# Routing of a two-layer graph and expert kernel done row tile by row tile

## The chip, the cores and the metric

The kernel runs on one core of one Trainium2 chip. The core has five engines that run side by side: PE (matrix multiplies), DVE (vector), ACT (activations, here also copies and a DMA queue), POOL (general, here also indirect DMA) and SP (which only issues DMAs). PE works on clocks that are granted to it, 2.4 GHz or 1.2 GHz. The metric is the device time of one execution in microseconds, the median of several.

## What is computed

N = 3327 nodes with D = 256 features, a dense 0/1 adjacency matrix, E = 8 experts of which each node takes two.

```python
x = x + L0_gnn(layernorm(x), adj)   # softmax(x @ node_w) * softmax(where(adj > 0, h @ h.T, -big)), times adj, @ (x @ weight) + bias
x = x + L0_ffn(layernorm(x))        # top 2 of x @ Wg + bg; (silu(x @ W1) * (x @ W3)) @ W2 by expert, H = 512
x = x + L1_gnn(layernorm(x), adj)   # relu((adj @ x) @ W.T + b)
x = x + L1_ffn(layernorm(x))        # top 2 of x @ gate_w.T; gelu(x @ w1.T + b1) @ w2.T + b2 by expert, H = 1024

top_vals, top_idx = top_k(logits, 2)
gates = softmax(top_vals)           # y[node] = sum over its two experts of gate * expert(x[node])
```

## The kernel before

The nodes stand in T = 26 row tiles of P = 128 (the last has 127 rows). The program is a list of stages; at the end of each (`Stage.end`) all five engines meet at a barrier, so no engine starts on a stage before the slowest has left the one ahead. The order of the instructions is written out by hand, an engine at a time, and semaphores tie the engines together; `tiles` unrolls the first tiles and the last and loops over the rest two at a time. The stages are

- `project`: layernorm and the three projections. SP also turns both gate weights to expert-major rows in DRAM (`a["turned"]`).
- `attend`: for each row tile the scores against all nodes in seven chunks (PE L624), masked by DVE (L548), the exponential on ACT (L515); then in seven groups PE turns the probabilities (L633), ACT copies them as the high part (L521), DVE takes the low part (L533), and PE multiplies both with the support rows (L659, L661, the last one L664). The scores of tile t+1 run ahead of the groups of tile t.
- `route` (name gate0), `experts` (ffn0), `normalize`.
- `neighbours`: for each row tile PE turns the mask in four parts (L1417), ACT and DVE copy it (L1476, L1509), PE multiplies it with the normed nodes (L1424), turns the sum (L1433, function `finish` of PE) and projects it (L1439); DVE's `finish` adds bias, applies relu, adds x and takes the row statistics (L1519 to L185).
- `route` (gate1), `experts` (ffn1), `copy_out`.

The class `Gate` is called by both loops. POOL norms a finished row tile (L199 to L211), SP stores it to `xn`, and DVE forms the eight logits as eight products with sums over 256 columns (L224, `sums`) and adds the bias (L230) into `LG`, which holds all logits until `route`. In `attend` the eight sums of tile t−1 stand in twos between the low parts of the groups of tile t; in `neighbours` all eight of tile t−3 stand between the second and the third copy of the mask.

`route` then works on all 3328 x 8 logits at once: top two, gates, a count of the pairs before each pair (PE L804, L805), a place for every pair, and an inversion of that list by one-hot multiplies (L813), which yields `r["tok"]`, `r["dst"]`, `r["of_pair"]` and `r["expert"]` for S = 59 tiles of 128 pairs, sorted by expert. Meanwhile SP issues the weights: in gate0 16 pieces of w_in (L973) and w_out in one (L976); for ffn1 the pieces of w_in are issued in the neighbours loop, w_out and the biases in gate1.

`experts` takes the 59 tiles in turn: POOL gathers 128 rows of `xn` by token (L1063), PE turns them (L1101), ACT copies them (L1160, `copy_x`), DVE takes the low part (L1232), PE multiplies (L1112, L1136), and POOL adds the result to the rows of x (L1076). `xn` rows are 258 wide, since the two gates of a node ride behind its features.

## Time and profile before

| | us |
|---|---|
| median of 3 runs | 1818.52 |
| lowest, highest | 1814.2, 1821.43 |
| the profiled execution | 1819.35 |
| span of its profile | 1817.8 |
| PE, DVE, POOL, ACT busy in it | 1551.0, 1150.7, 698.9, 638.9 |

The span is the time between the first and the last instruction in the trace. The stages lie in it so: projection to 83 us, attention to 657, routing to 698, experts to 1026, normalize to 1066, neighbours to 1316, routing to 1357, experts to 1803, the copy of the output to the end. In a row of the timeline the first number is the start in us, the second the duration; a bracket says how long the engine stood idle ahead of it and what released it. A row with xN stands for N like instructions in a row.

### The profile page before, as it was taken

How to read it: one execution, taken by the hardware profiler on the slowest of the kernel's cores; microseconds unless marked ns; L12 is line 12 of the kernel's file. 1: busy time of each engine (PE TensorE's matmuls, PEld its weight loads, DVE VectorE, ACT ScalarE, POOL GpSimd, SP SyncE). 2: the span in 40 equal slices, each digit the busy share in tenths (PEclk: the TensorE clock that was granted, in tenths of full speed). 3: DMA queues.
4: the chain of work that ended last, by engine and by line, in shares of the span. 5: the costliest groups of instructions: out<-in, count | busy, mean ns of one | idle time of the engine just before them, and what ended most of it. 6: DMA issues, size and time to landing. Idle time of an engine off the chain costs nothing. (4 is left out here: it accounts for less than half of the span.)

```text
span 1817.8 us, 36040 instructions
## 1 busy us (share of the span) xinstructions
PE 1551.0 (85%) x9584; PEld 1291.5 (71%) x9584; DVE 1150.7 (63%) x3860; ACT 638.9 (35%) x1349; POOL 698.9 (38%) x1336
## 2 busy tenths in 40 slices
PE   5899999999999925999999339999618999999994
PEld 4888888888888724887888326555307888888894
DVE  5467777777777776566655346666685666666652
ACT  2333333333333301322223243222205565555562
POOL 0122322232222213776667204443414555455551
PEclk9899999999999966999999769999858999999997
DMA  6324344333334353333333424555341222222223
GB/s 94 111 109 150 136 145 151 132 130 130 130 132 146 98 196 114 51 49 49 52 49 50 98 94 153 195 205 195 110 189 30 41 35 38 38 35 36 40 37 91
DMA packets 85363, 184.70 MB, mean 102 GB/s; under 512 B 19790, under 2 KB 62540, under 8 KB 81292
## 3 DMA queue, kind: packets, MB, share of 16 engines
q1 hardware_dynamic: 57386, 128.02, 21.6%
q0 software_dynamic: 22656, 31.07, 11.2%
q10 hardware_dynamic: 5280, 25.17, 3.5%
q8 instruction: 14, 0.23, 0.1%
q14 instruction: 27, 0.21, 0.0%
HBM read 132.66 MB, written 54.99 MB: 103 GB/s over the span
## 5 line engine op out<-in xcount | busy, mean ns | idle before, releaser
L1112 PE MATMUL bank<-ffn_w_in_parts,ffn_x_t 128*128 128x512 f32 x1416 | 361.1, 403 | 1.7 <-DVE ffn_w_in_parts L1251 1.7
L1136 PE MATMUL bank<-ffn_w_out_parts,ffn_hidden_t 128*128 128x256 f32 x2124 | 285.0, 288 | 19.5 <-DVE ffn_hidden_t L1241 19.5
L1112 PEld LDWEIGHTS bank<-ffn_w_in_parts,ffn_x_t 128*128 128x128 f32 x1416 | 258.9, 190 | 55.9 <-DVE ffn_w_in_parts L1251 5.0
L1136 PEld LDWEIGHTS bank<-ffn_w_out_parts,ffn_hidden_t 128*128 128x128 f32 x2124 | 263.2, 192 | 25.1 <-issue 16.2
L624 PE MATMUL bank<-h_t,attn_h_tile 128*128 128x512 f32 (+1 forms) x1092 | 248.8, 383 | 3.9 <-POOL attn_h_tile L493 3.9
L659 PE MATMUL bank<-support,attn_probs_t 128*128 128x512 f32 x650 | 246.7, 413 | 5.1 <-DVE attn_probs_t L533 4.7
L624 PEld LDWEIGHTS bank<-h_t,attn_h_tile 128*128 128x128 f32 x1092 | 197.0, 189 | 46.1 <-issue 4.1
L521 ACT CAST attn_probs_t<-bank 128x512 fp32r<-128x512 f32 (+1 forms) x182 | 98.7, 557 | 357.5 <-PE bank L633 357.5
L1076 POOL DMA_INDIRECT x<-ffn_y,ffn_dst x118 | 196.5, 1665 | 53.6 <-issue 53.6
L1178 ACT ACTIVATE ffn_silu_or_gelu<-bank,w_b_in 128x128 f32<-128x128 f32 x472 | 134.6, 368 | 155.9 <-PE bank L1123 155.9
L661 PE MATMUL bank<-support,attn_probs_t 128*128 128x256 f32 x676 | 185.0, 280 | 0.0
L533 DVE TENSOR_TENSOR attn_probs_t<-bank,attn_probs_t 128x512 fp32r<-128x512 f32 (+1 forms) x182 | 116.1, 650 | 79.7 <-ACT attn_probs_t L521 79.0
L1424 PE MATMUL bank<-normed_parts,nbr_adj_t 128*128 128x512 f16 x676 | 164.7, 382 | 0.0
L1241 DVE TENSOR_TENSOR ffn_hidden_t<-ffn_silu_or_gelu,ffn_hidden_t 128x512 fp32r<-128x512 f32 x118 | 81.1, 692 | 129.3 <-ACT ffn_hidden_t L1184 127.3
L548 DVE CUSTOM_DVE_ANT_0 attn_scores<-bank,attn_mask 128x512 f32<-128x512 f32 (+1 forms) x182 | 116.0, 649 | 57.4 <-issue 57.3
L659 PEld LDWEIGHTS bank<-support,attn_probs_t 128*128 128x128 f32 x650 | 122.0, 188 | 31.7 <-DVE attn_probs_t L533 7.7
L1063 POOL DMA_INDIRECT ffn_x_gathered<-xn,ffn_tok x118 | 124.4, 1055 | 17.6 <-issue 4.8
L661 PEld LDWEIGHTS bank<-support,attn_probs_t 128*128 128x128 f32 x676 | 127.7, 189 | 1.1
L1123 PE MATMUL bank<-ffn_identity,ffn_hidden 128*128 128x128 f32 x708 | 97.4, 274 | 17.1 <-DVE ffn_hidden L1225 12.9
L1417 PE MATMUL bank<-nbr_identity,nbr_mask 128*128 128x128 bf16 x676 | 55.9, 222 | 65.5 <-DMA nbr_mask<-mask 63.2
L1417 PEld LDWEIGHTS bank<-nbr_identity,nbr_mask 128*128 128x128 bf16 x676 | 46.1, 99 | 85.7 <-issue 69.1
L224 DVE CUSTOM_DVE_ANT_0 attn_gate_products<-attn_x_normed,attn_gate_w 128x256 f32<-128x256 f32 x208 | 103.3, 534 | 3.4 <-issue 3.4
(248 smaller groups left out, 2388.5 us busy)
## 6 DMA issues: line engine op xcount, KB each, us to landing
adj_tile<-in_adj SPq DMA_DIRECT2D x25, 1663.5 KB, 7.6
mask<-attn_mask ACTq DMA_DIRECT2D x26, 832.0 KB, 3.4
nbr_mask<-mask SPq DMA_DIRECT2D x26, 832.0 KB, 5.1
w_w_in<-in_w SPq DMA_DIRECT2D x16, 512.0 KB, 10.5
w_w_in<-in_w_t SPq DMA_DIRECT2D x16, 512.0 KB, 4.2
w_w_out<-in_w SPq DMA_DIRECT2D x1, 4096.0 KB, 20.5
x<-attn_x_out SPq DMA_DIRECT2D x26, 128.0 KB, 1.7
xn<-attn_x_normed SPq DMA_DIRECT2D x26, 128.0 KB, 2.5
```

The costliest lines, as they stand in the source:

```text
L224: dve.tensor_tensor_reduce(out=self.PR[:, e, :], in0=self.XN[:, slot, :], in1=self.GW[:, e, :], scale=1.0, scalar=0.0, op0=ALU.mult, op1=A ...
L533: dve.tensor_tensor(PT[:, half(slot, g), 1, 0:gn * P], bank[4 + half(slot, g)][:, 0:gn * P], PT[:, half(slot, g), 0, 0:gn * P].bitcast(F32 ...
L548: dve.tensor_tensor_reduce(out=SC[:, slot, c0:c0 + cn], in0=bank[c % 4][:, 0:cn], in1=NEG[:, slot, c0:c0 + cn], scale=1.0, scalar=-3.0e38, ...
L624: ins = pe.matmul(bank[c % 4][:, 0:cn], HS[:, slot, hs, k, :], HT[:, hm, k, c0:c0 + cn], start=n == 0 and k == 0, stop=n == 2 and k == KD - 1)
L659: pe.matmul(bank[6 + slot][:, :], part[:, 0, :], SUP[:, jt, :, :].rearrange("p a d -> p (a d)"), start=jt == 0, stop=False)
L661: ins = pe.matmul(bank[6 + slot][:, 0:D], part[:, 1, :], SUP[:, jt, 0, :], start=False, stop=False)
L1063: pool.indirect_dma_start(out=XG[:, slot, :], out_offset=None, in_=a["xn"], in_offset=bass.IndirectOffsetOnAxis(ap=TOKS[:, slot:slot + 1], ...
L1076: pool.indirect_dma_start(out=acc, out_offset=bass.IndirectOffsetOnAxis(ap=DSTS[:, slot:slot + 1], axis=0), in_=YS[:, slot, :], in_offset= ...
L1112: ins = pe.matmul(bank[2 + 2 * slot + b][:, :], XT[:, slot, xp, k, :], WIP[:, wp, k, b * CH:(b + 1) * CH], start=n == 0 and k == 0, stop=n ...
L1136: ins = pe.matmul(bank[7][:, 0:D], HTT[:, hp, k, :], WOP[:, wp, k, :], start=n == 0 and k == 0, stop=n == 2 and k == KH - 1)
L1178: ins = act.activation(GATE[:, j, k * P:(k + 1) * P], src[:, k * P:(k + 1) * P], ACT.Gelu, bias=w.BI[:, bass.ds(e * KH + (4 * j + k), 1)])
L1424: ins = pe.matmul(bank[2 + slot][:, :], AT[:, g % 2, j * P:(j + 1) * P], XH[:, g0 + j, :, :].rearrange("p a d -> p (a d)"), start=g0 + j = ...
```

## The change

Both `route` stages are gone, and `LG` with them. The routing of a row tile is done inside the loop that makes the tile, by new functions of `Gate`:

- PE turns the normed rows (`flip_rows`, two 128x128 transposes), ACT copies them to SBUF (`copy_rows`), PE multiplies by the gate weights (`multiply_rows`).
- DVE adds the bias (`logits`), takes the top two and their indices and forms the two-hot row `USED` (`pick`); PE multiplies it with a triangle and with ones (`count`), which gives the pairs ahead of each pair in the tile and the total of the tile; DVE adds the running base and picks the place of either pair (`rank`); ACT takes the exponential (`exp`), DVE the gates (`gates`).
- POOL writes each pair (node and gate, 8 bytes) with two indirect DMAs (`scatter`) to a list in DRAM at expert * CAP + rank. The lists are filled with empty entries by SP in `project`.
- After the last tile DVE computes from the eight totals which expert and which row of the lists each of the 59 tiles has (`plan`, twelve operations on one partition).

`experts` loads the pairs of each tile from the lists by SP (`load_pairs`), and takes token, destination and gate from there. Weights are loaded by expert, by ACT, at the start of the expert stage ahead of its first `copy_x` (`w.load(act)`); expert 0's w_in of ffn0 is loaded in `attend`, and the pieces of w_in for ffn1 still come in the neighbours loop.

```diff
+    def multiply_rows(self, pe, t, slot):
+        pe.wait_ge(self.xnt_ready, t + 1)
+        for k in range(KD):
+            ins = pe.matmul(self.PS[slot][:, 0:E], self.XNT[:, k, :], self.GW[:, k, :], start=k == 0, stop=k == KD - 1)
...
+    def pick(self, dve, t, slot):
+        link(dve.max(self.M8[:, slot, :], self.L[:, slot, :]))
...
+        dve.tensor_tensor(self.DIFF[:, slot:slot + 1], self.M8[:, slot, 1:2], self.M8[:, slot, 0:1],
+                          ALU.subtract).then_inc(self.diff_ready, 1)
+        link(dve.max_index(self.I8[:, slot, :], self.M8[:, slot, :], self.L[:, slot, :]))
+        link(dve.tensor_copy(self.EF[:, slot, :], self.I8[:, slot, 0:2]))
+        link(dve.tensor_scalar(self.OH[:, slot, :], self.k["IE"][:], self.EF[:, slot, 1:2], None, ALU.is_equal))
...
+    def count(self, pe, t, slot, rows=P):
+        pe.wait_ge(self.used_ready, t + 1)
+        pe.matmul(self.PS[slot][:, E:2 * E], self.k["BEFORE"][0:rows, :], self.USED[0:rows, slot, :], start=True, stop=True)
+        pe.matmul(self.PS[slot][:, 2 * E:3 * E], self.k["ONES"][0:rows, :], self.USED[0:rows, slot, :],
...
 def attend: DVE
-                        if g - EARLY < 4 and not (first and slot == 0):
-                            gate.sums(dve, t - 1, 1 - slot, range((g - EARLY) * 2, (g - EARLY) * 2 + 2))
+                        score(t + 1, 1 - slot, first and slot == 0, lambda: rest(t, slot, range(EARLY)),
+                              {0: pick, 2: rank} if routed else {})
...
 def attend: PE
+                        scores(t + 1, 1 - slot, first and slot == 0, lambda: early(t, slot, first),
+                               {0: multiply_rows, 2: count} if not known(t) or t >= 2 else {})
...
+    def load(self, act):
+        for e in range(E):
+            if not self.early and (e > 0 or self.first is None):
+                act.dma_start(self.WI[:, :, e * m:(e + 1) * m], self.w_in[:, :, e * m:(e + 1) * m]).then_inc(self.in_loaded[e], 16)
+            act.dma_start(self.WO[:, :, e * D:(e + 1) * D], self.w_out[:, :, e * D:(e + 1) * D]).then_inc(self.out_loaded[e], 16)
...
 def experts: ACT
+                w.load(act)
                 copy_x(0, 0, 0)
...
 def neighbours: PE
+                    if not known(t) or t >= 4:
+                        gate.count(pe, t - 4, slot)
                     for g in range(G):
...
+                        if g == 0 and (not known(t) or t >= 3):
+                            gate.flip_rows(pe, t - 3, 1 - slot)
                         if g == 2 and not very_first:
                             project_out(t - 1, 1 - slot)
+                        if g == 2 and (not known(t) or t >= 3):
+                            gate.multiply_rows(pe, t - 3, 1 - slot)
...
 def neighbours: DVE
+                    if not known(t) or t >= 4:
+                        gate.rank(dve, t - 4, uses - 2, slot)
                     odd(t, slot, 1, first)
-                    if not known(t) or t >= 3:
-                        logits(t - 3, 1 - slot)
                     odd(t, slot, 3, first)
+                    if not known(t) or t >= 4:
+                        gate.gates(dve, t - 4, uses - 2, slot)
                     if not very_first:
                         finish(t - 1, uses - (1 - slot), 1 - slot, first)
...
+                    if not known(t) or t >= 3:
+                        pick(t - 3, 1 - slot)
```

In `neighbours` the turned sums now use one PSUM bank (bank 4) in place of two, and the gate's work uses bank 5. The lines of the changed kernel are numbered anew: L1455 is the turned mask, L1462 the multiply, L1473 the turned sum, L1479 the projection.

On PE, one step of the neighbours loop, before:

```order
L1417 MATMUL bank<-nbr_identity,nbr_mask 128x128 x7
L1424 MATMUL bank<-normed_parts,nbr_adj_t 128x512 x7
L1417 MATMUL bank<-nbr_identity,nbr_mask 128x128 x6
L1424 MATMUL bank<-normed_parts,nbr_adj_t 128x512 x7
L1433 MATMUL bank<-nbr_identity_f,nbr_sum 128x128 x2
L1417 MATMUL bank<-nbr_identity,nbr_mask 128x128 x6
L1424 MATMUL bank<-normed_parts,nbr_adj_t 128x512 x6
L1439 MATMUL bank<-nbr_w_t,nbr_sum_t 128x256 x2
```

and after (L295 and L296 are `count`, L246 is `flip_rows`, L260 `multiply_rows`):

```order
L295 MATMUL bank<-nbr_pairs,k_before 128x8
L296 MATMUL bank<-nbr_pairs,k_ones 128x8
L1455 MATMUL bank<-nbr_identity,nbr_mask 128x128 x7
L1462 MATMUL bank<-normed_parts,nbr_adj_t 128x512 x7
L246 MATMUL bank<-nbr_identity_f,nbr_x_normed 128x128 x2
L1455 MATMUL bank<-nbr_identity,nbr_mask 128x128 x6
L1462 MATMUL bank<-normed_parts,nbr_adj_t 128x512 x7
L1473 MATMUL bank<-nbr_identity_f,nbr_sum 128x128 x2
L1455 MATMUL bank<-nbr_identity,nbr_mask 128x128 x6
L1462 MATMUL bank<-normed_parts,nbr_adj_t 128x512 x6
L1479 MATMUL bank<-nbr_w_t,nbr_sum_t 128x256 x2
L260 MATMUL bank<-nbr_gate_w,nbr_x_normed_t 128x8 x2
```

The step now opens with the count of tile t−4; the turned rows stand behind the first multiply, the gate multiply behind the projection.

On DVE, the end of one step of the neighbours loop, before (L230 ends the eight sums):

```order
L230 TENSOR_TENSOR logits<-nbr_logit_sums,nbr_gate_b 128x8
L1507 REGISTER_ALU
L1509 TENSOR_SCALAR nbr_adj_t<-bank 128x768
L1519 TENSOR_TENSOR nbr_before_relu<-bank,nbr_bias 128x256
L1520 REGISTER_ALU
L1522 ISA
L1525 SCALAR_TENSOR_TENSOR nbr_x_out<-nbr_before_relu,nbr_x 128x256
L180 BN_STATS nbr_row_sums<-nbr_x_out 128x6
L184 MEMSET nbr_dve_wait_taker 128x1
L185 BN_AGGR nbr_mean_var<-nbr_row_sums 128x2
```

and after:

```order
L1584 SCALAR_TENSOR_TENSOR nbr_x_out<-nbr_before_relu,nbr_x 128x256
L204 BN_STATS nbr_row_sums<-nbr_x_out 128x6
L208 MEMSET nbr_dve_wait_taker 128x1
L209 BN_AGGR nbr_mean_var<-nbr_row_sums 128x2
L268 TENSOR_TENSOR nbr_logits<-bank,nbr_gate_b 128x8
L278 MEMSET nbr_dve_wait_taker 128x1
L279 MAX nbr_top<-nbr_logits 128x8
L282 TENSOR_TENSOR nbr_logit_difference<-nbr_top 128x1
L284 MAX_INDEX nbr_top_index<-nbr_top,nbr_logits 128x8
L285 CAST nbr_pair_expert<-nbr_top_index 128x2
L286 TENSOR_SCALAR nbr_second_hot<-k_iota_expert,nbr_pair_expert 128x8
L289 SCALAR_TENSOR_TENSOR nbr_pairs<-k_iota_expert,nbr_pair_expert,nbr_second_hot 128x8
```

The sums are gone from between the two copies of the mask, and a chain of short operations on eight columns stands behind the row statistics.

On ACT, the passage into the first expert stage, before:

```order
L821 ACTIVATE gate_top<-gate_top 128x26
L770 UNCONDITIONAL_BRANCH
L1154 UNCONDITIONAL_BRANCH
L1160 CAST ffn_x_t<-bank 128x256 x2
L1166 ACT_TABLE_LOAD
```

and after, the last rows ahead of the same copy:

```order
L993 DMA w_w_in<-in_w 128x2x1024
L994 DMA w_w_out<-in_w 128x4x256
L1190 CAST ffn_x_t<-bank 128x256 x2
L1196 ACT_TABLE_LOAD
L1196 ACTIVATE ffn_silu_or_gelu<-bank 128x512
```

Fifteen DMA issues, in alternation w_out and w_in, of which the last two are shown, stand between the barrier and the copy that the first multiply of the stage needs.

## Rows read from the trace of the kernel before

**Rows 1.** Windows: start:end length, busy us by engine, granted clock, DMA share, GB/s

```profile
108.00:626.00 518.00, 513.98 (x2896) 441.02 (x2895) 366.44 (x1426) 167.98 (x218) 148.83 (x287) 1.00 0.38 134
...
657.00:698.00 41.00, 7.96 (x54) 4.40 (x54) 36.58 (x121) 0.23 (x1) 1.71 (x12) 0.50 0.87 308
...
1075.00:1304.00 229.00, 214.68 (x1492) 128.13 (x1489) 147.91 (x635) 63.03 (x102) 87.97 (x250) 0.99 0.51 172
```

**Rows 2.** All of L664, last matmul of a tile: ns, first and last start

```profile
L664 PE MATMUL bank<-support,attn_probs_t x26: 394/398/398, 116.6 to 647.4; 128*128 128x512 f32 x26
```

**Rows 3.** Timeline, PE, an attention tile: start, us, operation, [idle <-releaser]

```profile
303.25 0.50 PE L659 MATMUL bank<-support,attn_probs_t 128*128 128x512 f32 x1 [0.34 <-DVE attn_probs_t L533]
...
306.60 0.38 PE L633 MATMUL bank<-attn_identity,attn_scores 128*128 128x128 f32 x2
306.76 0.50 PE L659 MATMUL bank<-support,attn_probs_t 128*128 128x512 f32 x1
...
308.97 7.16 PE L624 MATMUL bank<-h_t,attn_h_tile 128*128 128x512 f32 x30
```

**Rows 4.** Timeline of PE in one neighbours tile

```profile
1192.68 0.56 PE L1417 MATMUL bank<-nbr_identity,nbr_mask 128*128 128x128 bf16 x7 [0.63 <-DMA nbr_mask<-mask]
...
1198.34 0.50 PE L1417 MATMUL bank<-nbr_identity,nbr_mask 128*128 128x128 bf16 x6
1198.67 1.46 PE L1424 MATMUL bank<-normed_parts,nbr_adj_t 128*128 128x512 f16 x6
```

**Rows 5.** Timeline of DVE in the same attention tile

```profile
307.84 0.15 DVE L572 RECIPROCAL attn_small<-attn_small 128x1 f32<-128x1 f32 x1
308.12 0.22 DVE L574 SCALAR_TENSOR_TENSOR attn_small<-attn_small,attn_node_attention 128x1 f32<-128x1 f32 x1
...
319.63 0.16 DVE L553 TENSOR_REDUCE attn_small<-attn_max 128x1 f32<-128x7 f32 x1
319.83 0.15 DVE L556 TENSOR_SCALAR attn_small<-attn_small 128x1 f32<-128x1 f32 x1
```

**Rows 6.** Timeline, all engines, end of attention to first experts

```profile
647.36 0.40 PE L664 MATMUL bank<-support,attn_probs_t 128*128 128x512 f32 x1
...
652.31 0.56 POOL L211 TENSOR_SCALAR attn_x_normed<-attn_x_out,attn_rstd 128x256 f32<-128x256 f32 x1
...
698.87 0.31 POOL L1049 MEMSET ffn_zero<- 128x256 f32 x1 [40.16 <-POOLq L102]
...
705.62 0.37 ACT L1160 CAST ffn_x_t<-bank 128x256 fp32r<-128x256 f32 x1 [41.96 <-PE bank L1101]
...
707.41 4.49 PE L1112 MATMUL bank<-ffn_w_in_parts,ffn_x_t 128*128 128x512 f32 x12
```

**Rows 7.** Timeline of SP, then all of L973: ns min/median/max, starts

```profile
656.93 16.11 SPq L973 DMA_DIRECT2D w_w_in<-in_w  x16
...
L973 SPq DMA_DIRECT2D w_w_in<-in_w x16: 595/1001/1597, 656.9 to 671.7; - x16
...
L973 SPq DMA_DIRECT2D w_w_in<-in_w_t x16: 593/598/646, 1141.5 to 1274.5; - x16
```

**Rows 8.** DMA rate in 40 slices, 657:672 us, then 1028:1040

```profile
GB/s 0 0 0 38 104 186 311 382 393 344 371 410 311 246 251 284 279 262 218 257 279 322 355 360 393 410 421 404 399 421 404 382 410 371 393 382 399 377 388 393
...
GB/s 0 0 31 123 58 106 276 389 365 324 345 369 352 273 259 300 341 379 379 372 348 382 352 358 345 341 355 348 341 358 341 355 345 341 355 348 317 246 133 34
```

**Rows 9.** All stores of x in the neighbours loop, L1374

```profile
L1374 SPq DMA_DIRECT2D x<-nbr_x_out x26: 332/355/356, 1091.4 to 1307.5; - x26
```

**Rows 10.** Timeline of DVE in the same neighbours tile

```profile
1192.09 0.42 DVE L1519 TENSOR_TENSOR nbr_before_relu<-bank,nbr_bias 128x256 f32<-128x256 f32 x1 [1.15 <-PE bank L1439]
...
1193.57 0.18 DVE L185 BATCH_NORM_AGGREGATE nbr_mean_var<-nbr_row_sums 128x2 f32<-128x6 f32 x1
```

**Rows 11.** Timeline, all engines, start of the second experts

```profile
1358.28 0.31 POOL L1049 MEMSET ffn_zero<- 128x256 f32 x1 [40.48 <-POOLq L102]
...
1367.56 5.42 PE L1112 MATMUL bank<-ffn_w_in_parts,ffn_x_t 128*128 128x512 f32 x12
```

More of the change, by code:

```diff
@@ L605, in _, with scores @@
                 link(dve.tensor_scalar(NATT[:], NATT[:], NSM[:, 3:4], None, ALU.mult))
-                tiles(dve, T, step)
-                gate.sums(dve, T - 1, (T - 1) % 2, range(E))
-                gate.logits(dve, T - 1, (T - 1) % 2)
+                tiles(dve, T, step, head=4)
+                for t in (T - 2, T - 1):
+                    gate.logits(dve, t, t % 2)
+                    gate.pick(dve, t, t % 2)
+                    gate.rank(dve, t, t // 2, t % 2)
+                    gate.gates(dve, t, t // 2, t % 2)
+                gate.plan(dve)
             @block.tensor
             def _(pe):
-                def scores(t, slot, first, midway=None):
+                def scores(t, slot, first, midway=None, behind={}):
                     pe.wait_ge(h_ready, t + 1)
@@ L1461, in _ @@
                 pe.wait_ge(w_loaded, 32)
-                tiles(pe, T, step)
+                tiles(pe, T, step, head=4)
             @block.scalar
```

618 lines of the change are left out of this document (327 added, 291 removed).

## The prediction, made before the changed kernel ran

> **What bounds the kernel now.** I read first the table of windows, which cuts the span at the stage borders. In the attention loop PE is busy 513.98 of 518 us, in the loop over neighbours 214.68 of 229: what is added to PE there lengthens the span. In the first routing stage ACT stands still, PE works 7.96 us and DVE 36.58 of 41, and the second is the same code; nothing of the next stage can run there, so both are pure gaps [rows 1]. Then I read one tile of each loop, to see which engine hands over to which [rows 2 to 5, 9, 10], the timelines of both gaps, for what the last tile's gate waits for and what the expert stage does before its first real matmul [rows 6, 11], and SP's queue, for the price of weight loads [rows 7, 8]. The profiled execution took 1819.35 us; the median of the runs is 1818.52, 0.8 less. The sum is made against the first.
>
> **Attention loop.** One tile takes (647.4 − 116.6) / 25 = 21.23 us [rows 2]. Per tile PE gets two f32 transposes, two f32 multiplies with 8 columns (two passes each, four records) and two bf16 counts. Two transposes cost 0.16 us from their start to the next start [rows 3]. The eight-column passes have no row. They need the same weight loads as the six bf16 ones that take 0.33 us together [rows 4], 0.055 each, and f32 doubles that: 0.11 each, 0.45 in all, is my value. Counts 0.11, and 0.15 for the break in the weight prefetch on the way in and out: 0.9 us. DVE loses eight sums of 0.35 us, which sit here between the corrections of the probabilities; PE waited 0.34 us behind such a correction [rows 3]. I give back 0.5 us per tile for that. The count for tile t−2 waits for DVE's pick: eight short operations, seven of them each waiting for the one before. Chained short ones start 0.20 us apart [rows 5], so the pick takes 1.5 us after DVE has masked the first chunk of scores. In that time PE has two chunks of scores, 1.4 us each by 7.16 us for 30 records of six each [rows 3], less what DVE lags, and arrives about 0.2 us early. Sum 0.9 − 0.5 + 0.2 = +0.6 per tile, 25 tiles: **+15**. Bounds: +3, if the break is free and the handovers all return; +30, if the chained operations start 0.3 us apart.
>
> **First gap.** Before: the last matmul starts at 647.36, the tile is normed at 652.87, then come its eight sums, barrier and routing, and the expert stage begins at 698.87 [rows 6]. After: normed 652.87, transposes 0.7 (PE has stood idle, and the clock granted in this gap is 0.50, the 1.2 GHz level [rows 1]), copy 0.4, multiply 0.8, pick 1.5, count 0.3, rank 1.2, gates 0.6 → 658.4. The plan is twelve chained operations on one partition, some over 59x8, estimated at 0.34 each: 4.1 us → 662.5. The last scatters land within that; with the barrier the stage begins at 664.5. Gain 34.4.
> But the weight loads move. SP issued 16 loads of 512 KB while the routing ran; now ACT issues 15 loads, 11 MB, **ahead of its first copy_x**, and PE's first multiply waits for that copy. SP needed 16.11 us for its 16, 1001 ns in the median, though the same line in the neighbours loop, with an empty queue, needs 598 [rows 7]: the issuing engine is held while the queue is full. The transfer ran at some 390 GB/s once begun [rows 8]. In 16.11 us, 1.7 of them start-up, 5.6 MB had gone of 8.4, so about 3 MB stand in the queue when the last issue returns, and ACT is free after (11 − 3) / 0.39 = 20.5 us, 21 with the start. From the copy to the first matmul it is 705.62 to 707.41, 1.8 us [rows 6]. So the first expert matmul comes 22.8 us after the stage's begin; before it came at 707.41 − 698.87 = 8.5. Net 14.3 − 34.4 = **−20**. Bounds −34 (ACT not held) and −17 (only 2 MB held, the 1 KB runs of w_out slower).
> Here the Trainium skill speaks the other way: "DMA: Bandwidth & Descriptors", section "Issuing engines are not separate DMA queues", says that all issuers share the 16 engines and that the time to initiate a DMA is usually small beside the transfer itself. By that ACT would be free after a few us and the sum would be that of rival A; in this trace a full queue held the issuer 1.0 us per 512 KB.
>
> **Neighbours loop.** A tile takes (1307.5 − 1091.4) / 25 = 8.64 us [rows 9]. DVE's finish runs from 1192.09 to 1193.75, released by PE's projection, and nobody waits for it soon [rows 10]. After, the pick of tile t−3 is queued behind the finish, and the count of it opens PE's next step. Between the projection and that count PE has only multiply_rows 0.45, transposes 0.33 and multiplies 1.30 [rows 4]: about 2.1 us. DVE needs for the same way finish 1.65, a gap of 0.13 and logits and pick 1.5: 3.3. So PE stands 1.1 to 1.2 us in front of the count, once per tile, and has 0.9 of own work more. The wait for the mask (0.63 before one transpose [rows 4]) falls in part into the new one: −0.5. Sum +1.5 per tile; 21 tiles have the whole of it: **+31**. Bounds +7 (the pick is over before PE comes, 0.3 us of own work) and +45 (pick 2.2 us). ACT's added copy and exp, POOL's added scatter (an operation, a taker, two issues) and SP's unchanged list fit a period of 10 us: 0.
>
> **Second gap.** Before: expert stage 1358.28, its first big matmul 1367.56, 9.3 later [rows 11]. The last store of x starts at 1307.5 [rows 9]; after, the last finish ends near 1308.2, the places of tile t−3 near 1310, and the three last tiles go one after another through transpose, copy, multiply, pick, count, rank and gates, 4.15 us each: 1322.5; plan 4.1, landing and barrier 2 → 1328.5 on the old clock. Gain 29.8. ACT now issues 9 MB, w_out in 1 KB runs and the biases; runs of 1 KB moved at about 345 GB/s [rows 8], and 2 MB of them stand in the queue: (9 − 2) / 0.345 = 20.3 us, with start and copy 22.3 in place of 9.3. Net 13.0 − 29.8 = **−17**. Bounds −28 and −12.
>
> **The rest.** The expert loops lose a 0.15 us DVE operation per tile, off PE's path; SP's loads of pairs run far ahead: −1. Projection loses four turning DMAs and gains the filling of the lists, both under PE's work, which ends the stage: 0, and if the lists' 0.5 MB came last, +2.
> Sum: 15 − 20 + 31 − 17 − 1 = **+8**: 1827.4 profiled, 1827 as a median.
>
> **Rivals.**
> *A. ACT is not held.* If ACT's queue takes 15 loads in 7 us (0.35 to 0.6 each, the price with an empty queue [rows 7]), copy_x follows when the gather has landed anyway. Both gaps then give −34 and −28 in place of −20 and −17, and about 1 comes back where expert 1 waits for its weights: −24 → **1803**. Against it: the median of 1001 ns of a full queue.
> *B. The pick is off PE's path among the neighbours.* The count's wait shrinks to nothing and the period is 8.9 in place of 10.1: −25 → **1802**. For it: DVE has 81 us free in that loop [rows 1]. Against it: the order on DVE, not its load, makes the wait. A and B together: 1779.
> *C. Slower.* The chained short operations of the pick start 0.3 us apart instead of 0.2, the maximum and its index being those without a row; the pick takes 2.2 us and PE waits 0.6 more at each count: 14 among the neighbours, 15 in attention, 3 in the tails → **1859**. It decides from a pick above 1.7 us. For it: a small division and its follower start 0.28 apart in the same loop [rows 5].
>
> **Chances.** Forecast 0.49, A 0.16, B 0.12, both 0.05, C 0.18. A measurement of this kernel tells about 0.5% from no change, so "same" is 1809.4 to 1827.6. The forecast's own spread (1815 to 1838) lies a little over half inside: 0.28 same, 0.21 slower. A, B and both are faster, 0.33; C is slower, 0.39 with the forecast's part. The range runs from 1798 (A or B alone) to 1855 (the lower part of C).
>
> **What would show it.** Attention: the last matmuls of the tiles lie 21.8 us apart. First gap: ACT's issues take 20 us in a row, PE's first expert matmul comes about 23 us after the barrier; under A they take 7. Neighbours: the stores of x lie 10.1 us apart, with PE idle before the count, released by DVE's pairs; under B 8.9 and no such wait. Under C the pick, from logits to pairs, takes over 2 us. What would break it: a wait that I take to be covered, above all the chain from count over rank to the next tile's transposes, which share one PSUM bank with them.

## The result and the profile after

| us | before | after |
|---|---|---|
| median, before beside after on the same chip | 1819.13 | 1843.02 |
| lowest and highest | 1814.2, 1821.43 | 1838.07, 1844.33 |
| the profiled execution | 1819.35 | 1838.07 |
| span of its profile | 1817.8 | 1836.2 |

The ratio after to before is 1.0129, with 95% between 1.0107 and 1.0151: the change makes the kernel slower by 1.3%, 24 us in the medians. The profiled execution of after is the lowest of its four, so the spans differ by less, 18.4 us; the working below is made on these 18.4. A second profile of the same kernel, `r1` below, lies 4 us higher with the same stages, a little in each.

The table cuts each span at the same events: the last matmul of the first and of the last attention tile, the begin of an expert stage (its first instruction on any engine), the first expert matmul, the first and the last store of x among the neighbours. "Gap" is from the last event of the loop to the begin of the expert stage.

| us | before | after | difference | forecast |
|---|---|---|---|---|
| attention, 25 tiles | 530.8 (21.23 each) | 546.1 (21.84) | +15.3 | +15 |
| gap 1 | 51.5 | 21.6 | −29.9 | −34.4 |
| begin of experts 1 to first matmul | 8.5 | 25.1 | +16.6 | +14.3 |
| experts 1, normalize, to the first store of x | 384.0 | 382.9 | −1.1 | |
| neighbours, 25 tiles | 216.1 (8.64) | 243.8 (9.75) | +27.7 | +31 |
| gap 2 | 50.8 | 26.6 | −24.2 | −29.8 |
| begin of experts 2 to first matmul | 9.3 | 25.4 | +16.1 | +13 |
| the rest, with the start | 566.8 | 564.7 | −2.1 | −1 with the stretch above |

**Windows of after**, in the columns of [rows 1]: the same stretch of the attention loop, the first gap, the neighbours loop.

```profile
108.00:626.00 518.00, 516.64 (x3010) 444.52 (x3010) 327.71 (x1330) 178.75 (x259) 204.12 (x387) 1.00 0.37 133
...
663.50:684.70 21.20, 2.45 (x13) 1.69 (x12) 10.48 (x55) 0.78 (x3) 7.79 (x20) 0.57 0.04 13
1092.00:1336.00 244.00, 217.17 (x1582) 137.55 (x1579) 129.61 (x626) 70.60 (x145) 119.88 (x353) 1.00 0.47 155
```

In the same 518 us of attention PE is busy 2.7 us more than in [rows 1], with DVE 39 us less busy; PE was the bound and stays it. In the 244 us of neighbours PE is busy 217.17, 27 less than the window, where before it was 14 less than the window. What PE waited for in the 25 tiles (us in all, times, longest), before and then after:

```profile
PE bank L1417 <- DMA nbr_mask<-mask: 10.4, 11, 1.7
```

```profile
PE bank L295 <- DVE nbr_pairs L289: 25.0, 22, 1.3
```

All its waits together are 14.7 us before and 26.4 after.

**All last matmuls of an attention tile and all stores of x**, after (duration ns, first and last start; they answer to [rows 2] and [rows 9]):

```profile
L875 PE MATMUL bank<-support,attn_probs_t x26: 394/394/398, 117.0 to 663.1; 128*128 128x512 f32 x26
```

```profile
L1404 SPq DMA_DIRECT2D x<-nbr_x_out x26: 332/355/357, 1092.7 to 1336.5; - x26
```

(663.1 − 117.0) / 25 = 21.84 and (1336.5 − 1092.7) / 25 = 9.75.

**PE in one neighbours tile of after**, from the projection to the count (answers to [rows 4]):

```profile
1228.68 1.03 PE L1479 MATMUL bank<-nbr_w_t,nbr_sum_t 128*128 128x256 f32 x4
1229.54 0.51 PE L260 MATMUL bank<-nbr_gate_w,nbr_x_normed_t 128*128 128x8 f32 x4
1229.91 0.55 PE L1455 MATMUL bank<-nbr_identity,nbr_mask 128*128 128x128 bf16 x7
1230.30 1.46 PE L1462 MATMUL bank<-normed_parts,nbr_adj_t 128*128 128x512 f16 x6
1232.83 0.18 PE L295 MATMUL bank<-nbr_pairs,k_before 128*128 128x8 bf16 x1 [1.08 <-DVE nbr_pairs L289]
```

**DVE in the same tile** (answers to [rows 10]):

```profile
1229.74 0.42 DVE L1578 TENSOR_TENSOR nbr_before_relu<-bank,nbr_bias 128x256 f32<-128x256 f32 x1 [1.08 <-PE bank L1479]
...
1231.33 0.13 DVE L268 TENSOR_TENSOR nbr_logits<-bank,nbr_gate_b 128x8 f32<-128x8 f32 x1
1231.51 0.17 DVE L279 MAX8 nbr_top<-nbr_logits 128x8 f32<-128x8 f32 x1
...
1232.55 0.23 DVE L289 SCALAR_TENSOR_TENSOR nbr_pairs<-k_iota_expert,nbr_pair_expert,nbr_second_hot 128x8 bf16<-128x8 f32 x1
```

PE has its projection, the gate multiply, one part of the mask and one set of multiplies, and then stands 1.08 us until DVE's pairs (L289) come. DVE begins the finish when the projection is there, at 1229.74, and works to 1232.78 with no wait for another engine; the pick from the logits' start to the pairs' end is 1.45 us.

**All engines, from the end of attention into the first experts**, after (answers to [rows 6]; 684.72 is the first instruction of the expert stage):

```profile
663.07 0.40 PE L875 MATMUL bank<-support,attn_probs_t 128*128 128x512 f32 x1
...
668.03 0.55 POOL L235 TENSOR_SCALAR attn_x_normed<-attn_x_out,attn_rstd 128x256 f32<-128x256 f32 x1
...
676.32 0.96 POOL L353 DMA_INDIRECT pairs<-attn_pair_values,attn_place_int  x1 [0.30 <-issue]
...
677.86 0.21 DVE L379 TENSOR_TENSOR route_row<-attn_plan_row,k_iota_tile 1x59 int32<-1x59 f32 x1
...
684.72 0.20 POOL L1082 MEMSET ffn_identity<- 128x128 f32 x1 [7.44 <-POOLq L106]
...
708.47 0.37 ACT L1190 CAST ffn_x_t<-bank 128x256 fp32r<-128x256 f32 x1 [36.82 <-issue]
...
709.76 2.48 PE L1142 MATMUL bank<-ffn_w_in_parts,ffn_x_t 128*128 128x512 f32 x5
```

The last matmul starts at 663.07, the tile is normed at 668.58, the pairs are formed at 672.34, the plan ends at 678.07. Then nothing computes for 6.6 us. Among the queue instructions of the block's end stand these (first gap, second gap):

```profile
L599 DVEq DRAIN  x1: 17/17/17, 678.3 to 678.3; - x1
...
L599 POOLq DRAIN  x1: 4308/4308/4308, 679.0 to 679.0; - x1
...
L1399 POOLq DRAIN  x1: 4317/4317/4317, 1357.8 to 1357.8; - x1
```

DVE has reached the end at 678.3; POOL's drain (an instruction of its queue that ends the block) starts at 679.0, behind POOL's wait for the last scatters to land, and takes 4.31 us, and the barrier waits for it. In the second gap the plan ends at 1356.13, POOL's drain takes 4.32 us and the stage begins at 1363.08, 7.0 us after DVE's last operation. In before, the drain of POOL at the end of attention, and the two at the end of the expert stages, which have indirect DMAs on POOL too (at the end of the two routing stages, without indirect DMAs, POOL's drain took 1.5 us):

```profile
L429 POOLq DRAIN  x1: 842/842/842, 652.1 to 652.1; - x1
...
L1040 POOLq DRAIN  x2: 2104/2105/2106, 1024.4 to 1800.9; - x2
```

**ACT's issues of weights in after** (one row for each line and source; ns min, median, max, first and last start; they answer to [rows 7]):

```profile
L993 ACTq DMA_DIRECT2D w_w_in<-in_w x7: 708/3219/4505, 685.3 to 704.4; - x7
...
L994 ACTq DMA_DIRECT2D w_w_out<-in_w x8: 582/638/904, 684.7 to 707.8; - x8
L994 ACTq DMA_DIRECT2D w_w_out<-in_w_t x8: 557/3009/6679, 1363.1 to 1384.2; - x8
```

w_in of an expert (1 MB) takes 3.2 us to issue in the median, up to 4.5, and the first copy of ACT comes at 708.47, 23.75 us after the stage's begin. The engines that carry the DMAs are busy 98% of that time and move 339 GB/s (last two columns), 8.0 MB in all:

```profile
684.73:708.47 23.74, 0.66 (x2) 0.29 (x2) 3.77 (x4) 0.00 (x0) 6.23 (x11) 0.50 0.98 339
```

### The profile page after: what moved, and what is told of

Its sections match the earlier page's. It is cut to its first block and busy times, and to the rows that moved or that the text cites. A ratio compares the mean times of both kernels' runs of the same rounds, so it can differ in the third digit from the quotient of the medians.

```text
span 1836.2 us, 38087 instructions
## 1 busy us (share of the span) xinstructions
PE 1574.2 (86%) x9892; PEld 1321.1 (72%) x9892; DVE 1034.7 (56%) x3501; ACT 663.5 (36%) x1451; POOL 809.0 (44%) x1580
## 3 DMA queue, kind: packets, MB, share of 16 engines
q0 software_dynamic: 25984, 31.06, 10.4%
## 5 line engine op out<-in xcount | busy, mean ns | idle before, releaser
L1166 PEld LDWEIGHTS bank<-ffn_w_out_parts,ffn_hidden_t 128*128 128x128 f32 x2124 | 261.2, 191 | 24.2 <-issue 16.0
L824 PE MATMUL bank<-h_t,attn_h_tile 128*128 128x512 f32 (+1 forms) x1092 | 259.2, 386 | 4.0 <-POOL attn_h_tile L663 4.0
L1462 PE MATMUL bank<-normed_parts,nbr_adj_t 128*128 128x512 f16 x676 | 164.2, 381 | 0.0
L1091 POOL COPY ffn_tok<-ffn_pairs 128x1 int32 (+1 forms) x118 | 92.9, 787 | 37.0 <-PE bank L1131 29.3
L1131 PE MATMUL bank<-ffn_identity,ffn_x_gathered 128*128 128x128 f32 x236 | 46.1, 278 | 73.4 <-DMA ffn_x_gathered<-xn,ffn_tok 46.6
L1462 PEld LDWEIGHTS bank<-normed_parts,nbr_adj_t 128*128 128x128 f16 x676 | 62.2, 98 | 56.0 <-issue 1.4
```

What stands on the lines that cost most here:

```text
L824: ins = pe.matmul(bank[c % 4][:, 0:cn], HS[:, slot, hs, k, :], HT[:, hm, k, c0:c0 + cn], start=n == 0 and k == 0, stop=n == 2 and k == KD - 1)
L1166: ins = pe.matmul(bank[7][:, 0:D], HTT[:, hp, k, :], WOP[:, wp, k, :], start=n == 0 and k == 0, stop=n == 2 and k == KH - 1)
L1462: ins = pe.matmul(bank[2 + slot][:, :], AT[:, g % 2, j * P:(j + 1) * P], XH[:, g0 + j, :, :].rearrange("p a d -> p (a d)"), start=g0 + j = ...
```

## The experiments

Each was timed beside the kernel before on the same chip; the medians of before there lay between 1815.99 and 1820.0. r1 and e1 to e3 share one chip, e4 to e7 a second, e8 and e9 a third, e10 and e11 a fourth; a difference of a few us between medians of different chips says little by itself, and there the stretches of the profiles are compared.

### r1: the changed kernel again

No edit.

> The changed kernel once more, unchanged. Its profiled execution took 1838.07 us, its three others 1842 to 1844. If the 5 us between them is chance of one execution, the time is again 1838 to 1845 and the stage borders of a second profile lie within 1 us of the first (experts at 684.7 and 1363.1 from the start); if one stage varies, its length shows which.

1842.64, ratio 1.0117 [1.0091, 1.0143], profiled 1842.0. Periods 21.89 and 9.75, gaps 21.9 and 26.5, first matmuls 25.5 and 26.7 after the stage's begin. The stage pattern repeats, and what follows is compared with this one as well.

### e1: the weights issued by SP

```diff
 def experts: SP
+    def step(t, *rest):
         load_pairs(t, *rest)
+        if known(t) and 1 <= t <= E:
+            w.load(sp, [t - 1])
+    tiles(sp, S, step, head=E + 2)
 def experts: ACT
-    w.load(act)
     copy_x(0, 0, 0)
```

> One part undone in another way: the weights of the experts are issued by SP, expert by expert between the loads of pairs, so that ACT copies the first rows at once. Theory (ACT is held by a full queue): the first expert matmul comes 9 to 12 us after the stage's begin in place of 25.0 and 25.4, and the kernel takes 1843 - 28 = 1815 (1810 to 1822). Rival (the transfer itself is what is waited for: the gather shares the DMA engines with 11 MB of weights and landed only 11 us after the begin, and expert 0's w_out and expert 1's w_in arrive late): the first matmul comes after 12 us but the next tiles wait for weights, and less than half comes back, 1830 to 1838.

1825.38, ratio 1.0016 [1.0001, 1.0032]: −17.3 in the medians against r1, −17.5 in the profiled executions, where 28 was expected (the range, 1810 to 1822, is missed). The first matmul comes 12.9 and 14.2 us after the begin in place of 25.5 and 26.7, so 25 us of hold are gone at the two places, but the stretch behind gives 6 back at the first (389.6 against 383.4). The timeline of POOL's gather and of PE at the start of the first experts (stage begin 685.6) shows why:

```profile
689.65 1.03 POOL L1100 DMA_INDIRECT ffn_x_gathered<-xn,ffn_tok  x1 [0.15 <-issue]
...
696.55 0.66 PE L1136 MATMUL bank<-ffn_identity,ffn_x_gathered 128*128 128x128 f32 x2 [23.20 <-DMA ffn_x_gathered<-xn,ffn_tok]
...
726.83 0.44 PE L1136 MATMUL bank<-ffn_identity,ffn_x_gathered 128*128 128x128 f32 x2 [2.26 <-DMA ffn_x_gathered<-xn,ffn_tok]
```

The gather's issue is over at 690.68 and its rows are there at 696.55: 5.9 us, against 1.9 at the same place in the kernel before, where the weights had been loaded during the routing. Later tiles' transposes wait 1.41 and 2.26 us for their gathers too. The hold of ACT was most of the cost, as the theory said; the rest looks like the rival's (the gather comes late beside the weights), which e6 tests.

### e2: the count one multiply later

```diff
 def neighbours: PE
-    gate.count(pe, t - 4, slot)
     for g in range(G):
...
-        if g == 0: gate.flip_rows(pe, t - 3, 1 - slot)
+        if g == 0: gate.count(pe, t - 4, slot)
         if g == 1: finish(t - 1, 1 - slot, first)
+        if g == 1: gate.flip_rows(pe, t - 3, 1 - slot)
 def neighbours: DVE
-    gate.rank(dve, t - 4, uses - 2, slot)
     odd(t, slot, 1, first)
+    gate.rank(dve, t - 4, uses - 2, slot)
```

(Conditions on the first tiles are left out; ACT's `copy_rows` and `exp` move behind its copies of the mask and of the turned sums.)

> Only the order in the loop over neighbours changes: PE counts the pairs of tile t-4 behind its first multiply and turns the rows of tile t-3 behind the second; DVE ranks behind its first copy of the mask; ACT copies the turned rows after both of its copies. Theory (the wait for the pick, 1.1 us per tile, is what the order makes): the period goes from 10.0 to 8.9 us, -24 us: 1819 (1815 to 1824). Rival (the period is set by the added work or by POOL's longer step, and the wait only moves elsewhere): within 6 us of 1843.

1820.2, ratio 1.0003 [0.9985, 1.0022]: −22.4 against r1. PE's count in one tile, and the stores of x:

```profile
1194.03 0.17 PE L295 MATMUL bank<-nbr_pairs,k_before 128*128 128x8 bf16 x1
...
L1404 SPq DMA_DIRECT2D x<-nbr_x_out x26: 333/355/372, 1094.0 to 1314.6; - x26
```

The count starts with no wait ahead of it, and the period falls from 9.75 to 8.82, 0.18 over before, which is less than the own work that PE got (0.9 us by the forecast, about 0.7 by the account further down): the rest fills what was idle, as PE now waits 4.9 us for the mask in the loop and not 10.4. So 23 us of the slowdown hung on where one instruction stands.

### e3: both edits

> Both edits, the loads by SP and the later count. If the two are independent, their gains add: by my theories 1843 - 28 - 24 = 1791 (1783 to 1800), faster than the kernel before the change; by the two rivals 1825 or more.

1802.3, ratio 0.989 [0.9869, 0.991]. The two gains add (−40.3 against −17.3 − 22.4); the time lies 11 us above the expectation and just outside its range; 10 of that is what e1 had already fallen short of. With two orders changed the design is faster than the kernel before by 1.1%.

### e4: the last scatters left out

The pairs of the last two row tiles (256 nodes) are never written in either loop, so POOL is done before DVE's plan.

```diff
-    gate.scatter(pool, T - 2, (T - 2) // 2, T % 2)
-    gate.scatter(pool, T - 1, (T - 1) // 2, (T - 1) % 2)
-    pool.wait_ge(self.scattered[slot], T // 2 * 32)
+    pool.wait_ge(self.scattered[slot], (T // 2 - 1) * 32)
```

> The changed kernel without the writes of the last two tiles' pairs to the lists, in both loops (8 indirect DMAs left out, the pairs of those 256 nodes are missing; counts and plan stay). It asks what the 4.3 us are that POOL's drain at the end of both stages takes after the last scatter (4308 and 4317 ns; 842 and 833 ns at the same places before, 2093 at the end of the experts). Theory (the drain waits for what the last indirect DMAs leave behind, so it runs off while DVE still works on the last tiles): POOL's last scatter ends some 4 us earlier among attention's tail, the drain lies beside DVE's plan, and the next stage begins 1 to 2 us after DVE's last operation instead of 6.6 and 7.0: about 10 us less in all, 1833. Rival (the drain costs a fixed 4.3 us from the end of the block in any stage with scatters, whenever they were, or the time is the barrier's): the stages still begin 5 us or more after DVE's last operation and the time is within 3 us of 1842.

1831.9 (one run). Drains at the end of attention and the first instruction of the experts:

```profile
L599 POOLq DRAIN  x1: 4554/4554/4554, 670.4 to 670.4; - x1
...
L599 DVEq DRAIN  x1: 17/17/17, 680.6 to 680.6; - x1
...
681.66 0.35 SPq L1075 DMA_DIRECT2D ffn_pairs<-pairs  x1
```

The drain is no shorter, 4.55 us (3.99 in the second gap), but starts at 670.4 and is over long before DVE reaches the end at 680.6; the stage begins 1.0 us later in place of 6.4. The gaps are 16.3 and 20.9 us in place of 21.6 and 26.6: −5.3 and −5.7, of which the omitted scatters' own landing is a part (1.7 us lie in after between the last issue's end, 677.28, and the drain). That is about what the forecast of the two gaps was off by before the ACT part (4.5 and 5.6). The run shows that the drain costs nothing where POOL is done early. That it is the scatters which make it three to five times as long as in before (0.84 and 1.5) is a comparison of kernels; no run here leaves them all out.

### e5: the gate multiply twice

```diff
-        for k in range(KD):
+        for n in range(2 * KD):
+            k = n % KD
```

> The changed kernel with the multiply by the gate weights issued twice as long in each tile: the same two products of 8 columns, then again (the first result is overwritten, the output is the same). It prices the eight-column passes, of which no row of before showed one. By the prediction four records cost 0.45 us: +11 us in the attention loop (26 tiles, PE-bound there), and up to +11 among the neighbours, less if the wait for the count, 1.1 us per tile, absorbs it. Rival: the passes are cheap since the weights of the next load beside them (0.2 us): +5 in attention. If the wait absorbs it, the neighbours' period stays at 9.75 us.

1851.68 (one run), +9.0 over r1. The last matmuls of the tiles:

```profile
L876 PE MATMUL bank<-support,attn_probs_t x26: 394/394/397, 116.9 to 672.1; 128*128 128x512 f32 x26
```

Attention: 22.21 per tile, +0.32 over r1 and +0.36 over after, so four more eight-column f32 records lengthen the tile by 0.34 us. That is less than PE spends on them. The stretch of PE from the first chunk of scores to the first turned probabilities holds the gate multiply and the counts and little else that is new; over 22 tiles (140 to 640 us) it takes 7.00 us in before, 7.15 in e10 below, which has the counts alone, 7.60 in after where PE does not wait, and 8.05 here. One tile each of before (its scores start at 308.97, [rows 3]), of e10 and of after:

```profile
315.97 1.03 PE L633 MATMUL bank<-attn_identity,attn_scores 128*128 128x128 f32 x8
```

```profile
312.94 5.76 PE L870 MATMUL bank<-h_t,attn_h_tile 128*128 128x512 f32 x24
...
320.10 1.03 PE L883 MATMUL bank<-attn_identity,attn_scores 128*128 128x128 f32 x8
```

```profile
336.25 1.56 PE L824 MATMUL bank<-h_t,attn_h_tile 128*128 128x512 f32 x6
...
343.85 0.38 PE L839 MATMUL bank<-attn_identity,attn_scores 128*128 128x128 f32 x2
```

So the counts cost PE 0.15 us and the multiply 0.45, the first as much as the second: 0.11 for each record, as forecast. Of the 0.45 only 0.34 lengthens the tile, since the waits that PE still had in after, 0.05 at the count and 0.06 elsewhere per tile, are filled. Neighbours: 9.748 ((1346.6 − 1102.9) / 25), unchanged: there PE's wait for DVE's pairs falls from 25.0 to 15.1 us, 0.45 in each of 22 tiles, which shows again that the chain over DVE sets that loop. The two gaps grow by 1.1 and 2.5, at the lower clock (granted 0.59 and 0.50).

### e6 and e7: gathers ahead of the weights

As e1 and as e3, but SP starts on the weights only when the first two gathers have landed.

```diff
+        if known(t) and t == 3:
+            for n in gathered:
+                sp.wait_ge(n, 16)
+            w.load(sp, [0, 1])
+        if known(t) and 4 <= t <= E + 1:
+            w.load(sp, [t - 2])
-        if known(t) and 1 <= t <= E:
-            w.load(sp, [t - 1])
```

> Like the run with the loads by SP, but SP waits until the first two gathers have landed before it issues the first weights. In the run with the loads by SP the first gather landed 5.9 us after its issue ended, with 1.9 before, and two later gathers held PE 3.7 us. Theory (the weights' own traffic makes the gathers late): the first expert matmul comes 9 to 10 us after the stage's begin instead of 13.0 and 14.2, and the weights, now 5 us later, are still in time for most tiles: 1825 - 6 = 1819 (1815 to 1822). Rival (the data rate is what counts: what the gather wins, the late weights lose again): within 2 us of 1825.

> The loads by SP behind the first gathers, together with the later count among the neighbours. If the gain of waiting for the gathers is real it adds to the 1802 of both orders: 1796 (1792 to 1799). If it is not, 1800 to 1805. Either way faster than the kernel before the change, by about 1%.

1828.77, ratio 1.0052 [1.0034, 1.0071], and 1805.73, ratio 0.993 [0.9903, 0.9957]: in the medians 3.4 us slower than e1 and than e3, which ran on another chip. PE where it first waits in either expert stage of e6:

```profile
704.37 0.66 PE L1162 MATMUL bank<-ffn_identity,ffn_hidden 128*128 128x128 f32 x4 [2.09 <-DVE ffn_hidden L1260]
...
1383.03 1.97 PE L1162 MATMUL bank<-ffn_identity,ffn_hidden 128*128 128x128 f32 x8 [7.79 <-DVE ffn_hidden L1264]
```

The first matmul comes 9.0 and 8.6 us after the begin, as in the kernel before, but PE then waits 2.09 and 7.79 us for DVE's hidden rows; DVE itself had stood 3.41 and 6.47 us in front of the first w_out. The stretches behind grow to 393.7 and 457.3, from 389.6 and 449.6 in e1. Over the two stages e6 wins 9.5 us at the first matmuls and loses 11.8 behind them; e7 wins 9.4 and loses 9.9 against e3. What is taken from the gather's wait is added to the weights'. The theory that the gather's landing was the loss of e1 falls. Its rival (the rate of transfer counts) fits these sums, although both medians lie 2 us or less outside the ranges that it had given.

### e8: ACT keeps the weights, behind its first two copies

```diff
-    w.load(act)
     copy_x(0, 0, 0)
     copy_x(1, 0, 1)
+    w.load(act)
```

> The changed kernel with one thing moved: ACT issues the weights behind its first two copies of rows instead of ahead of them. Theory (ACT is held by its full queue for some 23 us, wherever the issues stand): the gathers now run without traffic, the copies are done 9 us after the stage's begin and PE's first matmul starts then, but ACT's first activation waits for the last issue, some 32 us after the begin, so the stage ends later than before, not earlier: +5 to +8 us in each of the two stages, 1852 to 1858. Rival (an issue costs 0.6 us and what counted was only the order in the queue): the first activation comes within 12 us of the copies and the kernel takes 1825 or less.

1850.7 (one run), just under the range of the theory. ACT at the start of the first experts (stage begin 686.8):

```profile
696.22 0.37 ACT L1190 CAST ffn_x_t<-bank 128x256 fp32r<-128x256 f32 x1 [1.30 <-PE bank L1131]
...
714.94 3.36 ACTq L993 DMA_DIRECT2D w_w_in<-in_w  x1
...
719.00 1.28 ACT L1196 ACT_TABLE_LOAD   x1 [22.41 <-issue]
720.29 0.60 ACT L1196 ACTIVATE ffn_silu_or_gelu<-bank 128x512 f32<-128x512 f32 x1
```

Both copies are over at 696.6, and the next thing ACT computes is 720.29, 33.5 us after the begin: the issues hold it for 22.4 us. PE's first matmul starts 9.0 us after the begin, then PE waits 20.4 us for the hidden rows. The operand is there, and ACT still cannot work: what held it in after was its own issues and not the gather. Moving only the copies ahead moves the wait and lengthens it: from the begin to the end of what follows, the two stages take 4.4 and 2.9 us more than in r1, where 5 to 8 each was expected.

### e9: logits in attention by DVE's sums again

e3, and in `attend` the eight sums of before in place of the turned rows and the gate multiply; they stand in twos between the low parts, as in before. For room in SBUF the early load of expert 0's w_in is dropped.

```diff
 def attend: DVE
         rest(t, slot, [g])
+        if g - EARLY < 4 and not (first and slot == 0):
+            gate.sums(dve, t - 1, 1 - slot, range((g - EARLY) * 2, (g - EARLY) * 2 + 2))
 def attend: PE
-        gate.flip_rows(pe, t - 1, 1 - slot)
-    {0: multiply_rows, 2: count}
+    {2: count}
 def attend: ACT
-        gate.copy_rows(act, t - 1, 1 - slot)
```

> The kernel of both orders (loads by SP, later count; 1802.3), with one part of the change undone in attention alone: the logits are again eight sums on DVE between its corrections, and PE neither turns the rows nor multiplies them there; pick, count, rank, scatter and plan stay per tile. It needs the room of expert 0's early w_in, which is therefore loaded in the expert stage. Theory (attention's +0.61 us per tile is PE's own added work, and DVE has the time): the period goes from 21.84 to 21.3 to 21.4, -11 to -13 us; the late w_in of expert 0 gives 3 to 5 back: 1794 (1790 to 1798). Rival (the sums and the pick together make DVE late for PE): 1802 or more, with PE waiting for the corrections or for the pairs in attention.

1797.08, ratio 0.989 [0.9864, 0.9915]. The median is 5.2 less than that of e3, but the kernel before beside it was 4.0 less too: the ratios are equal, and the attention loop has to tell. PE at the count of one tile, and the last matmuls:

```profile
316.58 0.18 PE L298 MATMUL bank<-attn_pairs,k_before 128*128 128x8 bf16 x1 [0.35 <-DVE attn_pairs L292]
...
L917 PE MATMUL bank<-support,attn_probs_t x26: 394/398/398, 117.2 to 658.3; 128*128 128x512 f32 x26
```

Attention 21.64 per tile: −0.26 against e3, 6.3 us in the loop, where 0.45 of multiply (e5) and about 0.2 of transposes have left PE; the latter from the timeline of PE in after, from the start of L246 to the next start:

```profile
311.67 0.38 PE L246 MATMUL bank<-attn_identity,attn_x_normed 128*128 128x128 f32 x2
311.89 0.38 PE L839 MATMUL bank<-attn_identity,attn_scores 128*128 128x128 f32 x2
```

So with the sums back on DVE PE loses about 0.4 us per tile. Most of that is in front of the count: PE waits 0.35 us there in this tile, and over 22 tiles the stretch of scores (see e5) takes 7.48 us where e10 below needs 7.15, 0.32 more; in e3 the same loss is 0.05.

### e10 and e11: the count one chunk of scores later

e9 and e3, with the count (and DVE's rank) behind the fourth chunk of scores in place of the third.

```diff
-    {2: count}                      {0: pick, 2: rank}
+    {3: count}                      {0: pick, 3: rank}
```

> The run with the sums by DVE, with count and rank in attention one chunk of scores later (behind the fourth, not the third). In that run attention's period was 21.64 us, not the 21.3 expected, and PE stood 0.35 us in front of the count in the tile looked at. Theory (the rest of attention's loss over the kernel before, 0.41 us, is this wait and the count's 0.1): the period goes to 21.3 us, -8 us, 1797.1 - 8 = 1789 (1786 to 1793). Rival (DVE, busy 77% there, is late in any order, and the wait only moves to the masks or the corrections): within 3 us of 1797.

> The run of both orders (logits by PE in attention), with the same shift of count and rank by one chunk. There PE reached the count after its own multiply of the gate and waited only some 0.15 us by the timeline. Theory (attention's +0.61 us is 0.15 of wait and 0.45 of PE's own work net): the period goes from 21.86 to 21.7 us, -4 us: 1798 (1795 to 1801). Rival (the wait was larger than the timeline shows, since PE's records are pipelined): -8 us or more, 1794 or less.

1791.95, ratio 0.9864 [0.9837, 0.9891], and 1797.8, ratio 0.9882 [0.9859, 0.9906]. The last matmuls, e10 and then e11:

```profile
L917 PE MATMUL bank<-support,attn_probs_t x26: 394/398/398, 118.7 to 657.1; 128*128 128x512 f32 x26
```

```profile
L875 PE MATMUL bank<-support,attn_probs_t x26: 394/394/398, 116.6 to 662.2; 128*128 128x512 f32 x26
```

21.54 per tile against 21.64 in e9: the loss in front of the count, 0.32 us per tile, is gone, but 0.2 comes back among the groups, where PE now waits 4.6 us in all for DVE's corrections (118 to 640 us) and waited 2.5. So the wait moved for the larger part, as the rival of e10 had it, though less than wholly. In e11 it is 21.82 against 21.90 in e3, and the same attention code gave 21.83 to 21.90 in after, r1 and e1 to e8 without e5: no gain is shown, and only 0.05 of wait was there to win.

e10 and e11 ran on one chip and differ by e9's edit alone: 5.9 us in the medians, 7.2 in the attention loop. This, and not e9 against e3, shows that the sums on DVE are the better choice there. e10 is the fastest of all kernels here, 1.4% under the kernel before. It still has 0.3 us per tile more in attention than before: 0.15 are the counts; the other 0.15 lies among the groups and stays open.

## Why the prediction was right and where it was wrong

The direction of the likeliest case was right (a small loss), and the range held the time, but the loss is more than twice the forecast: +18.4 on the profiled spans and +24 on the medians, where +8 stood. That the range held is in part luck: 1843 lies above the forecast's own spread (1815 to 1838), in the part that was put there for rival C, and what C describes did not happen.

**Attention, +15: +15.3.** The sum came out, by luck: three of its terms were wrong and cancel. Per tile the multiply is 0.45 as forecast (e5), the counts 0.15 and not 0.11, the transposes about 0.2 and not 0.16, the wait for the pick 0.05 and not 0.2. The break in the weight prefetch (0.15) does not show: the multiply that is put in costs no more than one that follows another (e5). And what the sums gave back is 0.2 and not 0.5: in the 500 us from 140 to 640 PE stood idle 6.6 us before and 1.4 after, 0.28 and 0.06 per tile. Together 0.45 + 0.15 + 0.2 + 0.05 − 0.22 = 0.63, against 0.61 measured (the idle time is all that PE stood still, put down to the sums by inference).

**Neighbours, +31: +27.7.** The mechanism is as forecast in each part: the finish ahead of the pick, the pick of 1.45 us where 1.5 stood, PE idle for 1.08 where 1.1 to 1.2 stood, in each of the 22 tiles that have a count ahead of them. What was mis-sized is PE's own work: of the 27.7 us, 11.7 are waits (14.7 to 26.4; 21 tiles of 1.15 − 0.5 make 13.7), and the other 16 are 0.7 per tile in 22 tiles, not 0.9. e2 took that wait away alone and 23 us with it, where rival B had put 25.

**First gap, −20: −13.3.** The chain over the last tile's gate ran to the plan's end in 15.0 us after the last matmul, and 15.1 was forecast (647.4 to 662.5). The step that failed is the next: **"the last scatters land within that; with the barrier the stage begins at 664.5"**, 2 us from the plan to the stage. It took 6.6. The scatters' landing was not wholly hidden by the plan (0.9 us), and behind it stood a cost that I had not set down at all, POOL's drain of 4.31 us at the block's end. The trace of before had a sign of it: the drain of 2.1 us at the end of the expert stages, where POOL had issued indirect DMAs, against 0.84 at the end of attention, where it had not. The forecast used neither, since neither stands on a line that the diff touches. e4 shows the price: with POOL done early the gap shrinks by 5.3.
The second part, ACT held, was right in kind and 2.3 us short in size: copy 23.75 us after the begin and matmul 25.1, where 21 and 22.8 stood. While ACT was held, 8.0 MB moved at 339 GB/s, 7.6 MB of them weights; the forecast had 8 MB at 390 GB/s. The rate is the term that was mis-sized: 390 GB/s was read off the upper slices of [rows 8], which dip to 218; over the whole run of the old w_in loads, start-up left out, it was 345 GB/s in before (last column):

```profile
658.60:673.04 14.44, 0.51 (x2) 0.14 (x2) 13.07 (x47) 0.23 (x1) 0.11 (x2) 0.50 0.97 345
```

The bound of −17 was meant for this and not wide enough, since the drain came on top.

**Second gap, −17: −8.1.** The same step twice: 7.0 us from the plan's last operation to the stage where "landing and barrier 2" stood, and 25.4 to the first matmul where 22.3 stood; 310 GB/s moved while ACT was held, and the forecast had 345. e4 gives 5.7 of it back.

**The rest, −1: −3.2.** It falls out of the expert stretches; no run isolates it.

**Rival A** (ACT is not held) is refuted by the rows of L993 and by e8. By "DMA: Bandwidth & Descriptors", section "Issuing engines are not separate DMA queues", of the Trainium skill, the queues of all issuers share the 16 engines and interleave: e1 agrees, where the gather of POOL took 5.9 us beside SP's weights. The same section calls the time to initiate a DMA usually small beside the transfer: the trace differs for a full queue, where a 1 MB issue on ACT took 3.2 us, about as long as 1 MB takes at 339 GB/s (2.9 us). Even without the hold (e1) the gain is 17 and not the 24 that A was given: rows and weights then come together, and in either order (e6, e7) something waits for them.

**Rival B** had the right price but not the right order: it takes an edit (e2) to come about. **Rival C** fell: the short operations of the pick start 0.15 to 0.27 us apart, the maximum and its index 0.18 and 0.15 behind the one ahead, and the whole takes 1.45 us.

**The miss in one line**: stage ends +4.5 and +5.6, ACT's hold +2.3 and +3.1, neighbours −3.3, the rest −2.2, attention +0.3: together +10.3 on the forecast of +8. The further 5 us of the medians is that the profiled execution was the fastest of its four; the forecast, which set both kernels' profiled times 0.8 from their medians, had no term for that.

## What to carry to other kernels

Where work is moved out of a stage into the loops, price the end of the stage anew: what its last engine still has to finish, and what that engine does at the block's end (a drain after indirect DMAs cost 4.3 us here, twice) is part of the chain once the long work that hid it has gone. Weight loads that fill a queue belong on an engine that nobody waits for, and a small chain that crosses two engines in a loop costs what stands behind it in program order, so that one place later for one instruction was worth 23 us here. A slower result of a large change may hide a faster design: with loads and count in another place the same design went from 1.012 to 0.989 of the kernel before (e3), and with the logits of one loop back on DVE and its count one chunk later to 0.986 (e10).

## What the runs showed of the hardware

- POOL's drain at the end of a block took 4.31, 4.32, 4.55 and 3.99 us where scatters by indirect DMA stood ahead of it, 2.1 at the end of the expert stages, and without indirect DMAs 0.84 at the end of attention and 1.5 at the end of the routing stages of before; it is not much shorter with an early start (e4), but runs beside the other engines then.
- An ACT queue that takes 11 MB in 15 issues held the engine for 23.7 us, while 8.0 MB moved at 339 GB/s; the issue of one megabyte took 3.2 us in the median, that of the first, into an empty queue, 0.7.
- The landing of one gather of 128 rows went from 1.9 us to 5.9 beside the weight loads of SP (e1), and 6.1 beside those of ACT (after); holding the weights back for it gained nothing (e6, e7).
- Four f32 records of 128x8 on PE take 0.45 us of PE's time (8.05 − 7.60 us of scores, e5 and after), two bf16 records of 128x8 take 0.15 (7.15 − 7.00, e10 and before), and two f32 transposes of 128x128 put in alone 0.22 from start to start.
